# A graph network's edge stages: gathers and fetches moved across stage ends on GpSimd, node places worked out where the counts are made

## What is computed

```python
h = relu(layernorm(x)); x = x + segment_sum(h[src] * e, dst) @ W.T + b          # weighted sum
# second layer: edge attributes (32 wide) pooled by SOURCE: sum, max, mean, then two matmuls
h = concat([seg_sum, seg_max, seg_mean, u]); x = x + relu(h @ W1 + b1) @ W2 + b2
# third layer: eight relations
msg = hw[etype, src] / deg[dst]; x = x + where(deg > 0, relu(0.2*h + 0.8*segment_sum(msg, dst)), h)
# fourth layer: attention, softmax over each destination's edges
x = x + elu(segment_sum(z[src] * a, dst))
```

## Time and profile before

| | us |
|---|---|
| median of 3 runs | 23762.77 |
| lowest and highest run | 23706.22, 23770.17 |
| the profiled execution, its own time | 23824.81 |
| its span, first to last instruction | 23823.1 |
| busy: POOL, DVE, PE, ACT | 13595.7, 7609.3, 4383.5, 4314.4 |
| stage one, from the start to the places stage | about 80 to 2330 |
| the sort | 2336 to 9696 |
| stage three | 9696 to 13523 |
| first layers | 13528 to 14208 |

### The profile page before, as it was taken

One profiled execution on the slowest core, in us unless ns is written; L12 is line 12 of the kernel. 1 busy time (PEld: TensorE's weight loads), 2 busy tenths in 40 slices (PEclk: granted clock), 3 DMA queues, 4 the chain that ended last, 5 costly groups with the idle time before them and its releaser, 6 DMA issues. The chain is left out here.

```text
span 23823.1 us, 124820 instructions
## 1 busy us (share of the span) xinstructions
PE 4383.5 (18%) x27708; PEld 3352.9 (14%) x27708; DVE 7609.3 (32%) x21403; ACT 4314.4 (18%) x11116; POOL 13595.7 (57%) x13464
## 2 busy tenths in 40 slices
PE   1111444444444444111111160000000000000000
PEld 0111333333333333100000040000000000000000
DVE  4544333333333333445544411111111222222223
ACT  0000222322223222122212111111111011010100
POOL 4444444344443444555555527777777677777775
PEclk9999655555555555555555555555555555555555
DMA  1111000000000000122222211111111211111111
GB/s 54 32 32 34 15 16 15 14 16 15 16 15 16 15 14 15 58 77 83 79 72 77 75 53 50 47 47 47 47 47 47 35 48 51 48 48 48 48 48 42
DMA packets 577236, 985.00 MB, mean 41 GB/s; under 512 B 307983, under 2 KB 359920, under 8 KB 541168
## 3 DMA queue, kind: packets, MB, share of 16 engines
q0 software_dynamic: 430432, 388.76, 7.7%
q10 hardware_dynamic: 34560, 436.30, 4.4%
q1 hardware_dynamic: 111760, 155.76, 2.2%
HBM read 458.42 MB, written 521.52 MB: 41 GB/s over the span
## 5 line engine op out<-in xcount | busy, mean ns | idle before, releaser
L685 POOL DMA_INDIRECT by_src<-sort_row,sort_place_i x3240 | 3147.1, 971 | 4129.7 <-DVE sort_place_i L729 3157.7
L344 POOL DMA_INDIRECT rel_G<-rel_table,rel_idx x3240 | 3473.4, 1072 | 1470.0 <-issue 1034.2
L344 POOL DMA_INDIRECT att_G<-att_table,att_idx x3240 | 3417.6, 1055 | 1095.5 <-issue 1095.5
L344 POOL DMA_INDIRECT wsum_G<-h_table,wsum_idx x2160 | 2047.4, 948 | 2653.0 <-ACT wsum_idx L557 1915.2
L716 DVE TENSOR_TENSOR sort_before<-pS,below_b 128x128 bf16<-128x128 f32 x3242 | 942.8, 291 | 4490.7 <-remote 3395.1
L828 PE MATMUL pG<-sort_counts,sort_lowTf 128*128 128x98 f32 x6484 | 2126.0, 427 | 0.0
L374 DVE TENSOR_TENSOR wsum_low<-iota_b,wsum_parts 128x3840 bf16<-128x3840 bf16 x216 | 896.6, 4151 | 2984.3 <-remote 2779.8
L575 PE MATMUL wsum_C<-wsum_high,wsum_low 128*128 128x98 bf16 x6480 | 783.4, 274 | 5217.2 <-issue 3395.7
L791 ACT COPY sort_lowT<-pT 128x128 bf16<-128x128 bf16 x3240 | 864.2, 267 | 4531.8 <-remote 1800.4
L828 PEld LDWEIGHTS pG<-sort_counts,sort_lowTf 128*128 128x128 f32 x6484 | 1611.3, 305 | 0.0
L846 PE MATMUL pT<-ident_b,sort_low 128*128 128x128 bf16 x3240 | 900.7, 278 | 2659.3 <-issue 1431.6
(11 more groups left out here) (394 smaller groups left out, 11856.3 us busy)
## 6 DMA issues: line engine op xcount, KB each, us to landing
scan_att<-att_S ACTq DMA_DIRECT2D x54, 1980.0 KB
scan_wsum<-wsum_S ACTq DMA_DIRECT2D x54, 1920.0 KB
scan_pool<-pool_S ACTq DMA_DIRECT2D x72, 1440.0 KB
scan_rel<-rel_S ACTq DMA_DIRECT2D x54, 1920.0 KB
pool_row<-by_src SPq DMA_DIRECT2D x36, 1485.0 KB
sort_feat<-in_attr SPq DMA_DIRECT2D x54, 960.0 KB
by_src<-sort_row,sort_place_i POOLq DMA_INDIRECT x3240
rel_G<-rel_table,rel_idx POOLq DMA_INDIRECT x3240
```

The costliest lines, as they stand in the source:

```text
L344: pool.indirect_dma_start(out=G[s][:, j, :], out_offset=None, in_=table, in_offset=bass.IndirectOffsetOnAxis(ap=idx[s][:, j:j + 1], axis=0 ...
L685: pool.indirect_dma_start(out=by_src, out_offset=bass.IndirectOffsetOnAxis(ap=place_i[s][:, j:j + 1], axis=0), in_=row[s][:, j, :], in_off ...
```

## The change

- Two tiles `lead_rows0` and `lead_rows1` and their semaphores are made once for stages one to three; they are the two G tiles of stage three. A function `gather_lead` gathers one chunk into one of them with indices straight from `src_all`, without a wait.
- Stage one's GpSimd program calls it for chunk 18 behind its last gather. The sort calls it for chunk 19, in the place where it gathered chunk 18; its index copy is gone. Stage three's GpSimd program begins with chunk 20.
- Behind its last gather in stage three, GpSimd waits for the last store of the pooled rows and for the last pooling step, and then issues the 98 fetches of pooled rows, into `H`. They are gone from the first layers. `H` is made at the start, stands in for the tile `V_pool`, and until then also holds the pooling scans' result.
- The places blocks are gone. Their two matmuls and ten VectorE steps stand at the end of TensorE's and VectorE's programs of the counting stage.

```diff
+        H = sb("H", [P, HT, D])
+        lead = dict(rows=[sb(f"lead_rows{s}", [P, L, D], c=early) for s in range(2)],
+                    gathered=[semaphore(f"lead_gathered{s}") for s in range(2)])
+
+        def gather_lead(pool, s, chunk):
+
+            for j in range(chunk * L, (chunk + 1) * L):
+                pool.indirect_dma_start(out=lead["rows"][s][:, j - chunk * L, :], out_offset=None, in_=h_table,
+                                        in_offset=bass.IndirectOffsetOnAxis(ap=src_all[:, j:j + 1], axis=0)
+                                        ).then_inc(lead["gathered"][s], 16)
...
-                G = ([ahead["rows"], sb(f"{NAME}_G1", [P, L, width], F32, c)] if ahead else slots("G", [P, L, width]))
+                G = lead["rows"] if pooled else slots("G", [P, L, width])
...
-                    if ahead:
-                        gather(0, 1)
-                    with pool.Fori(1 if ahead else 0, NC // 2) as i:
+                    with pool.Fori(1 if pooled else 0, NC // 2) as i:
                         for s in range(2):
                             gather(i, s)
+                    if counts and not pooled:
+                        gather_lead(pool, 0, c1)
+                    if pooled:
+                        pool.wait_ge(pstored, 16 + 32 * NC)
+                        pool.wait_ge(pstate_ready, NC + 1)
+                        fetch(pool, scan_pool, end_src, H, 1)
...
                     if counts:
+                        steps = Steps(dve, place_steps)
                         dve.wait_ge(counted, 1)
-                        v.tensor_copy(count[:], C[:, 0:HT])
+                        v.tensor_copy(count[:], C[:, 0:HT]).then_inc(count_ready, 1)
+                        dve.wait_ge(count_ready, 1)
+                        dve.wait_ge(prefix_ready, 1)
+                        steps.done(v.tensor_tensor_scan(tile_end[:], ones[:, 0:HT], total[:, 0:HT], 0.0, ALU.mult, ALU.add))
...
+                        pe.wait_ge(count_ready, 1)
+                        mm(within[:, 0:HT], below_b[:], count[:], start=True, stop=True)
+                        mm(total[:, 0:HT], ones[:], count[:], start=True, stop=True).then_inc(prefix_ready, 1)
-        def places(by, count, first, end, base):
...
-                    pool.wait_ge(index_ready, 1)
-                    for j in range(L):
-                        pool.indirect_dma_start(
-                            out=ahead["rows"][:, j, :], out_offset=None, in_=h_table,
-                            in_offset=bass.IndirectOffsetOnAxis(ap=ahead["index"][:, j:j + 1], axis=0)
-                        ).then_inc(ahead["gathered"], 16)
+                    gather_lead(pool, 1, lead_chunk)
                     issue(0, 0, None)
...
-                    v.tensor_copy(ahead["index"][:], src_all[:, NCH // 3 * L:(NCH // 3 + 1) * L]).then_inc(index_ready, 1)
...
-                V, VP = sb("V_wsum", [P, HT, D], c=c), sb("V_pool", [P, HT, D], c=c)
+                V, VP = sb("V_wsum", [P, HT, D], c=c), H
...
-                    fetch(pool, scan_pool, end_src, VP, 1)
                     fetch(pool, scan_wsum, end_dst, V, 0)
```

More of the change, by code:

```diff
@@ L236, in _, with gathered_layer @@
                 sp.wait_ge(s_table, 16 * (7 + NPC + 1))
-        def gathered_layer(kind, table, width, rows_out, c0, c1, index, counts=None, pooled=False, ahead=None, weights=None,
+        def gathered_layer(kind, table, width, rows_out, c0, c1, index, counts=None, pooled=False, weights=None,
                            carried=None):
@@ L267, in gathered_layer @@
                 index_ready, index_loaded = sem("index_ready"), sem("index_loaded")
-                gathered = [ahead["gathered"] if ahead and s == 0 else semaphore(f"{NAME}_gathered{s}") for s in range(2)]
+                gathered = lead["gathered"] if pooled else [semaphore(f"{NAME}_gathered{s}") for s in range(2)]
                 stored = [sem(f"stored{s}") for s in range(2)]
@@ L276, in gathered_layer @@
                 if counts:
-                    by, count = counts
+                    by, count, first, end, base = counts
                     side_all = src_all[:, 0:J] if by == "src" else dst_all[:, 1:J + 1]
@@ L284, in gathered_layer @@
                     C = ps(f"{NAME}_C", [P, 512], c=c)
-                    split, parted, oh_ready, oh_used, zeroed, counted, taken = (
-                        sem(n) for n in ("split", "parted", "onehot_ready", "onehot_used", "zeroed", "counted", "taken"))
+                    ones = sb(f"{NAME}_ones", [P, P], F32, c)
+                    flag, tile_end, last_place = (stat[:, n, :] for n in range(3))
+                    within, total = ps(f"{NAME}_within", [P, 512], c=c), ps(f"{NAME}_total", [P, 512], c=c)
+                    split, parted, oh_ready, oh_used, zeroed, counted, count_ready, prefix_ready, place_steps = (
+                        sem(n) for n in ("split", "parted", "onehot_ready", "onehot_used", "zeroed", "counted", "count_ready",
+                                         "prefix_ready", "place_steps"))
                 if pooled:
@@ L503, in _ @@
                     if counts:
+                        steps = Steps(dve, place_steps)
                         dve.wait_ge(counted, 1)
[L505 removed]
+                        v.tensor_copy(count[:], C[:, 0:HT]).then_inc(count_ready, 1)
+                        dve.wait_ge(count_ready, 1)
+                        dve.wait_ge(prefix_ready, 1)
+                        steps.done(v.tensor_tensor_scan(tile_end[:], ones[:, 0:HT], total[:, 0:HT], 0.0, ALU.mult, ALU.add))
+                        steps.done(v.tensor_tensor(tile_end[:], tile_end[:], total[:, 0:HT], ALU.subtract))
+                        steps.done(v.tensor_tensor(first[:], tile_end[:], within[:, 0:HT], ALU.add))
+                        steps.done(v.tensor_scalar(flag[:], count[:], 0.0, None, ALU.is_gt))
+                        steps.done(v.tensor_tensor(last_place[:], first[:], count[:], ALU.add))
+                        steps.done(v.tensor_scalar(last_place[:], last_place[:], -1.0 - EP, None, ALU.add))
+                        steps.done(v.tensor_tensor(last_place[:], last_place[:], flag[:], ALU.mult))
+                        steps.done(v.tensor_scalar(last_place[:], last_place[:], float(EP), None, ALU.add))
+                        steps.done(v.tensor_copy(end[:], last_place[:]))
+                        if base:
+                            steps.done(v.tensor_scalar(first[:], first[:], float(base), None, ALU.add))
                     if c1 < NCH:
@@ L520, in _ @@
                         act.sem_inc(ptaken, 1)
-                    if ahead:
+                    if pooled:
+                        act.sem_inc(index_ready, 1)
                         act.sem_inc(index_ready, 1)
@@ L524, in _ @@
                         act.wait_ge(index_loaded, 32)
-                    for s in range(1 if ahead else 0, 2):
+                    for s in range(2 if pooled else 0, 2):
                         nc.scalar.copy(idx[s][:], index[:, (c0 + s) * L:(c0 + s + 1) * L]).then_inc(index_ready, 1)
```

54 lines of the change are left out of this document (10 added, 44 removed).

## The result

The changed kernel takes 23785.4 us in the median where the kernel before took 23748.4 in the same comparison; the ratio is 1.0016, 95% interval 1.0009 to 1.0024. In a second comparison it was 23793.2 against 23763.6 (1.0016, 1.0007 to 1.0025). So the change costs some 30 to 37 us, which is under the 0.3% that the prediction calls measurable, though neither interval takes in 1; it had 47.

The account below looks back on a forecast made before the run. No engine was taken to be full in stage one: gather bursts slow TensorE and its signals. Terms +75 - 5 + 0 - 20 - 3 = +47 us on the runs' median 23763 gave 23810 us, range 23690 to 23890.

Parts of the forecast that it names:

- The lead gathers in stage one: Stage one's tail: 60 more gathers prolong the burst that slows TensorE beside chunk 16's counting; +75 us, bounds 0 and 84.
- The places: End of stage one: the places' steps now run under ScalarE's copy and store; -5 us.
- The sort: Sort stage: still 60 lead gathers before its first scatter, only an index-copy wait under 1 us gone; 0 us.
- Stage three: Stage three: chunk pattern starts one chunk earlier, last index copy at 13495 and not 13515.07; -20 us, bounds -75 and +65.
- fast, slow, fast from here: Stage three after chunk 0's index copy: 17 pairs of 216.4 us and one fast chunk of 54.65 us.
- The pooled fetch: End of stage three and first layers: fetch moved earlier, VectorE released 15 to 21 us earlier; net -3 us, bounds -20 and +30.
- the term against it: First layers: VectorE's opening group-loop work, formerly done under the second fetch, loses cover; passes of 15 us each.
- The sum: Whole kernel: +75 - 5 + 0 - 20 - 3 = +47 us; forecast 23810 us.
- Longer pairs: Rival, stage three: loop branch inside bursts costs each of 17 pairs up to 5 us; total +67 to +132; chance 0.20.
- The leads swallowed: Rival, stage one: chunks 16 and 17 absorb the lead burst; total -28 us, 23735; chance 0.18.
- NOTIFIC — the notification-queue block: Rule weighed: held-up records push back on engines, so the crawl and stage one's +75 would be absent from unrecorded runs.
- Full credit: Rival: each GpSimd instruction taken from a stage's start gives back 1.25 us; 23555 us; chance 0.12, partial credit included.

Follow-up runs that it names:

- the last run: Changed kernel plus 60 GpSimd iotas between chunk 17's gathers and stage one's lead gathers; 23753.6 us against 23750.7 for the kernel before, ratio 1.0001.
- the first trace: First profiled execution of the changed kernel, nothing further altered; it took 23746.8 us, 78 us less than the profiled execution of the kernel before.
- the run of the first set with iotas: Changed kernel with 60 GpSimd iotas replacing stage one's lead gathers, both leads in the sort; 17620.0 us against 17422.8 for the kernel before, ratio 1.0111.

## Why the prediction was right, point by point

**The lead gathers in stage one: +75, right.** 76.5 and 76.6 us in the two traces of the changed kernel by the interval of the index copies, with the 18.4 us of lag borrowed from the earlier trace rows met (18.4 and 18.7), and the one build more that I had allowed. Undoing the leads took the 75 us out again. The mechanism read from the earlier trace rows holds too (the indirect DMAs, by the last run), with one thing missing: the crawl has a start-up. When the same burst starts where the counting ends, it costs 44 us (2377.5 against 2333.6), and those are accounted for by GpSimd alone: its last gather ends at 2362.0, and the sort's first instruction comes 15.6 us behind that.

**The places (-5): right.** From the last copy of results to the sort, 19.9 us became 14.9.

**The sort (0): right**, though its trace seemed to say -88. That goes with the granted clock of that one execution (0.56 from 2600 to 9600 us, where the kernel before has 0.54); it is more than the whole -78 between the two profiled executions, which without the sort stand 10 us apart the other way.

**Stage three (-20): right in its sign and its pattern, too small.** Measured -34 to -47. The 17 waits and the 216.3 us pairs are as forecast. The failed step is "fast, slow, fast from here": I gave the first slow chunk the 161.8 us of all others, though the earlier trace rows have 151.5 for the first one before (9760.87 to 9912.35). It took 137.2, 147.8 and 140.8 us in three traces. In the first trace the burst begins at 9747.3, and TensorE does 120 matmuls at full pace beside it, up to 9804.3, before the crawl; in the next burst (9939.2) it does 86, up to 9955.5. That is about one group of thirty more, and one wait of VectorE less. So the start-up is no fixed time (57 us and 16); it looks like a stock of instructions that a quiet stretch fills up. That is read from the trace and was not tried by itself.

**The pooled fetch (-3): right sign, too small.** Measured -13 to -18. VectorE was let go at T + 271.5 (forecast 266 to 272), but that hit is luck, made of two errors that cancel. The first layers began at T + 134.0 and not at T + 121 to 126, since GpSimd's next instruction came 15.4 us behind its last fetch, which the forecast held at nothing; the second fetch was done at T + 264.7 and not 244 to 250. And the lag from there to VectorE was 6.9 us and not the 21.8 borrowed from the earlier trace rows, which stands behind 196 fetches in one stage. The step that made the gain too small is the term against it: I charged 15 to 21 us minus some 15 for opening work that would lose its cover, but from that release to the next stage it is 404.4 us where the earlier trace rows have 406.4; the opening steps got done under the second fetch as before, with one pass of the group loop.

**The sum.** Averaged over the traces, the sort begins 75 us later (70 forecast, the places in it), stage three is 41 us shorter and the seam behind it 15.5: +75 - 41 - 15.5 = +18.5 by the traces; the medians say +37 and +30, whose intervals together span +17 to +59. With the measured sizes of the two gains the forecast would have been some +14 (70 - 41 - 15.5), nearer to the traces than to the medians; the 12 to 18 us in between I can't place. So the medians' closeness to +47 is in part luck: two gains were taken 33 us too small in all, and something unplaced goes the other way.

**The rivals.** Longer pairs: fell, all pairs after the first are 216.3 us. The leads swallowed: fell here, in each recorded execution. The Trainium skill, "NOTIFIC — the notification-queue block", section 7.1, had been weighed as a cause for a crawl in recorded executions only. It is not refuted. The prediction set the agreement of runs and profile against it, but that says nothing: every execution that was timed has a span and a granted clock of its own on record, so none shows the kernel unrecorded. And the traces of the first kind, alone, lack most semaphore updates of a burst (148 of 960 on record, against 957). While TensorE crawls they hold 1.44 updates and 1.6 instructions of all engines for each us; but it is not simply a fixed rate of records, since in the sort of the same trace there are 16.7 for each us. A run without recording would decide it, and there is none; if the rule is the cause, the crawl, the +75 and the difference between the two kinds of chip may all be absent from an unrecorded execution. Full credit (each GpSimd instruction counts): wrong on this kind, and on the second kind right in its premise but not in its sign, since the moved instructions were covered where they had stood.

**On the second kind the change itself was not run.** Worked out: with one lead in each place the first scatter comes some 25 us before that of the kernel with two in the sort (stage one's tail covers 33 us of the burst, less some 8 for the block's end), all else being equal: 17575 - 25 = 17550, 127 us or 0.7% over the kernel before. That is an estimate from the runs.

## What to carry to other kernels

Moving work of an engine that idles is not free where it slows its neighbours: price it by what stands beside it in the new place, and look whether the same pattern (gather, crawl, catch up) is in the trace already, since it gives both the price and the lag. A burst is cheapest where the others have just finished (44 us here and not 75); even there the stage's end waits for it. When a slowdown has no releaser, look at what the trace has failed to record in that stretch before you put it down to the chip. A stage that is hidden behind a loop on one chip and not on another makes the same edit a gain of 15 us or a loss of 85, so ask of a hidden fetch what hides it before moving it.

## What was not expected of the hardware

- **Two kinds of chip under one name.** The kernel before took 23706 to 23825 us on the first kind (three comparisons) and 17420 to 17433 on the second (two chips), at much the same mean granted clock (0.565 to 0.575 in the profiled executions of the first, 0.558 to 0.570 in those of the second). The difference is in bursts of indirect DMAs. In the sort's span it is 7180 us against 4124, where GpSimd is the bound and the clock no longer matters: 4123.9, 4124.1 and 4124.2 us at 0.566, 0.558 and 0.564. Why chips differ is open. What else the traces show to differ is how much of the semaphores' updates they hold, 62,016 and 256,152, so it may be a difference of the recording and not of the work.
- **Beside a computing GpSimd, VectorE's small operations are slower; beside a gathering one hardly.** In the run of the first set with iotas, in time:

```profile
1449.80 0.26 DVE L535 TENSOR_TENSOR first_src<-stat,wsum_within 128x98 f32<-128x98 f32 x1
1450.09 0.95 DVE L537 TENSOR_SCALAR stat<-count_src 128x98 f32<-128x98 f32 x1
...
1452.54 0.83 DVE L541 TENSOR_SCALAR stat<-stat 128x98 f32<-128x98 f32 x1
1453.40 1.13 DVE L542 CAST end_src<-stat 128x98 int32<-128x98 f32 x1
```

The scalar forms and the cast take 0.83 to 1.13 us and not the 0.21 of the changed kernel, the operation on two tensors its usual 0.26. With both leads in stage one the same steps fall beside gathers and take 0.21 to 0.37 us. The Trainium skill, "SBUF — State Buffer", Who interferes with whom, says just that of the port pair that VectorE and GpSimd share: copies, casts and scalar forms can contend for it, an operation on two tensors only with a GpSimd instruction that reads SBUF, which an iota doesn't. The same section has it that this pair is the only contention and that TensorE waits for nobody; on the second kind the traces agree, on the first TensorE issues 108 matmuls beside a burst and not 181, and what it waits for no row tells.
- What the crawl is, stays open. A stock of instructions that runs out, and then one each 1.4 us, would look like slow fetching of instructions; but the earlier trace rows have no packet of the instruction queue in such a stretch. A store of records that fills up and then empties slowly would look the same, and would explain the lag that grows with the burst (9.7 us behind 60 gathers, 18.4 behind 120); that is argued and not shown.
- A block's end takes longer when GpSimd is its last engine, with a burst or without: on the second kind the sort begins 6.7 us behind the last of 180 gathers and 7.0 us behind the last of 60 iotas, and the first layers 10.3 us behind the last fetch. On the first kind it is 15.4 us there, and 15.6 behind the lead gathers of the last run. Where VectorE's steps came last, in the places stage before, the next stage began 0.9 us behind them.
